# The drain of the last tiles of a fused attention and feed-forward layer: order, split copies, last layer norm

## The chip, the cores and the metric

The kernel runs on one core of one Trainium2 chip, as one launch. The time is the device time in microseconds, the median of several executions. TensorE (PE) multiplies, VectorE (DVE), ScalarE (ACT) and POOL (GpSimd) work element by element, SyncE (SP) issues the loads and stores of the token tiles. Each engine runs its own instructions in the order in which they were written, and waits on semaphores for the others.

## The reference

Input x is 16 x 512 tokens of width 256 in float32, 8192 tokens in all. All is float32.

```python
def favor(x):                       # per head of 16
    p = jnp.exp(x - jnp.max(x, axis=-1, keepdims=True))
    return p / (jnp.sum(p, axis=-1, keepdims=True) + 1e-6)

def fp4_linear(x, w):               # blocks of 16 along the last axis
    return jnp.einsum('bsk,nk->bsn', fp4_quant_dequant(x), fp4_quant_dequant(w))

x = layernorm(x + attention(x, Wq, bq, Wk, bk, Wv, bv, Wo, bo))   # linear attention on favor(q), favor(k)
h = jax.nn.silu(fp4_linear(x, w_gate)) * fp4_linear(x, w_up)      # width 704
x = layernorm(x + fp4_linear(h, w_down))                          # (x - mean) / sqrt(var + 1e-5)
```

`fp4_quant_dequant` scales each block of 16 by its largest absolute value over 6, rounds to the grid 0, 0.5, 1, 1.5, 2, 3, 4, 6 with its sign, and scales back. It is applied to the activations x and h as well as to the weights.

## The kernel before

The tokens are cut into 64 tiles of 128 (NT = 64), named n or, in sets of four, by sequence. The program has an attention part, which ends at about 240 us, and a feed-forward part. The array `res` holds the whole residual stream, 128 partitions x 64 tiles x 256, from the attention on. Every engine's program is written by one loop over steps m (`run`), and in a step each engine does one stage of several tiles: in step m of the feed-forward part TensorE does gate and up projections of tile m - 1 (in two halves, L974 and L996), the transposes of x of tile m (L981), the six transposes of the quantised hidden tile m - 4 (L992) and the down projection of tile m - 5 (L1001 to L1005). So steps 65 to 70 work off the last tiles, with ever fewer stages.

The way of one tile n from its hidden values to the output is the following, with the lines of the profile:

- VectorE finds the block maxima and their reciprocals (L759 to L769); POOL multiplies (L445); ScalarE squares and makes from it the rounding grid `hmg` (L606, L615); POOL adds the grid (L435) and VectorE subtracts it again (L808), which rounds to the FP4 grid; POOL multiplies by the scales (L416).
- TensorE transposes the six chunks into the PSUM tensor `wide` (L992). ScalarE copies them to `hqt_hi` rounded to the matmul's format (L594), VectorE subtracts that from `wide` to get the rest, `hqt_lo` (L814), and ScalarE copies a 64-row tail once more (L618, semaphore `h_dup`). The next tile's transposes wait for L618, since it reads `wide`.
- TensorE accumulates 17 matmuls of 128x256 into `bank5` (`pd`; L850, called by L1001, and L1003, L1005). It waits for `y_s`, the addition of the tile before, which frees the bank.
- VectorE adds the result to the residual and leaves the row sum (L772, `y_s`). ScalarE sums the squares about the mean (L492, `y_sq`).
- The layer norm's factors `rstd` and `nbias` are computed on VectorE for a batch of tiles at once, in thirteen small dependent steps (L643 to L657: an integer estimate of the inverse root, three Newton steps, the bias). The batches and the steps of the loop at which their operations stand are in `LN_B`: tiles 0 to 31, 32 to 47, 48 to 55, 56 to 59 and 60 to 63. The last starts at step 70, when the squares of tile 63 are there.
- ScalarE normalises each tile (L497) into one of four buffers `o_t`, and SyncE stores it (L336). `ready` spreads the normalisations of a batch over the steps behind its factors. They stand at the head of a step, ahead of the copy L594 of the same step. A normalisation also waits for the store that last read its buffer.

## Time and profile before

| what | value |
|---|---|
| median of 3 runs | 693.11 us (692.76 to 693.99) |
| the profiled execution | 694.08 us, its span 692.4 us |
| busy over the span | PE 673.5, DVE 634.7, ACT 572.7, POOL 575.9 us |
| granted TensorE clock, mean | 0.993 of full speed |
| stores | 64 of 128 KB, 1.7 us (median) from issue to landing |

The profile is of one execution. Its span is the time from the first to the last recorded event. Busy time is the sum of an engine's instructions; the chain of waits follows back from the last instruction what released each; a granted clock of 1.00 is 2.4 GHz. In the rows below a start is given in us from the span's start, and neighbouring instructions of one engine may overlap by about 0.1 us.

```profile
PE 673.5 (97%) x5586; PEld 640.9 (93%) x5586; DVE 634.7 (92%) x1499; ACT 572.7 (83%) x1356; POOL 575.9 (83%) x583
PE   8999999999999899999999999999999999999993
DVE  5999999999999879998999999899999999999884
ACT  6899999987779968898777768777777999888896
```

These are the busy times and 40 slices of the span, each digit the busy share of 17.3 us in tenths. The last slice is the drain of the pipeline.

### The profile page before, as it was taken

What the parts mean: (1) busy time and instruction counts of PE and PEld (TensorE: products, weight loads), DVE (VectorE), ACT (ScalarE), POOL (GpSimd) and SP (SyncE); (2) the same over time, 40 slices, a digit from 0 to 9 for tenths busy, and PEclk for the clock granted to TensorE, in tenths of its full rate; (3) what the DMA queues carried; (4) which work ended last, traced back from release to release, by engine and by line L of the source; (5) the groups of instructions that cost most, each with busy time, mean ns of one, the idle gap of its engine ahead of it and who ended that gap; (6) DMA issues with size and microseconds to landing.
All of it is one profiled execution on the core that took longest, in us unless ns stands there. A gap on an engine that the chain in (4) does not pass through costs nothing.

```text
span 692.4 us, 18052 instructions
## 1 busy us (share of the span) xinstructions
PE 673.5 (97%) x5586; PEld 640.9 (93%) x5586; DVE 634.7 (92%) x1499; ACT 572.7 (83%) x1356; POOL 575.9 (83%) x583
## 2 busy tenths in 40 slices
PE   8999999999999899999999999999999999999993
PEld 5899999999888799999999999999999999999983
DVE  5999999999999879998999999899999999999884
ACT  6899999987779968898777768777777999888896
POOL 5888888888888759998898899889878999888760
PEclk9999999999999999999999999999999999999998
DMA  5332323232331000000000000000000111101213
GB/s 159 101 91 75 98 73 92 84 94 78 92 91 58 18 1 0 3 1 1 1 2 1 2 1 1 2 1 1 2 1 2 46 40 39 47 32 47 69 60 116
DMA packets 40053, 29.87 MB, mean 43 GB/s; under 512 B 3731, under 2 KB 39958, under 8 KB 39958
## 3 DMA queue, kind: packets, MB, share of 16 engines
q1 hardware_dynamic: 37216, 26.49, 12.5%
q10 hardware_dynamic: 2742, 2.23, 1.1%
q8 instruction: 45, 0.74, 0.4%
q14 instruction: 50, 0.41, 0.2%
HBM read 20.32 MB, written 8.39 MB: 41 GB/s over the span
## 4 chain that ended last, share of the span: by engine, by line
PE 82%; issue 5%; POOL 5%; ACT 4%; DVE 3%; DMA 1%; ACTq 0%; SPq 0%; POOLq 0%; DVEq 0%
PE bank L850 62%; PE wide L992 6%; PE wide L850 5%; PE bank L981 2%; PE bank L932 2%; PE wide L950 1%; PE bank L912 1%; POOL scratch L399 1%; POOL scratch L374 1%; PE bank L1005 1%; PE bank L1003 1%; POOL rounded L391 1%; ACT scratch L497 1%; ACT dump L492 1%; DMA scratch<-L_attn_Wk 1%
## 5 line engine op out<-in xcount | busy, mean ns | idle before, releaser
L850 PE MATMUL bank<-wf_hi,rounded 128*128 128x352 f32 (+1 forms) x1664 | 387.2, 311 | 1.9 <-DVE res L772 1.7
L850 PEld LDWEIGHTS bank<-wf_hi,rounded 128*128 128x128 f32 x1664 | 284.4, 190 | 3.0 <-DVE rounded L814 1.7
L850 PE MATMUL bank<-wf_lo,rounded 128*128 128x352 f32 (+1 forms) x832 | 255.4, 307 | 0.0
L850 PEld LDWEIGHTS bank<-wf_lo,rounded 128*128 128x128 f32 x832 | 157.9, 190 | 0.0
L850 PE MATMUL bank<-qkv_hi,rounded 128*128 128x512 f32 (+1 forms) x512 | 144.7, 349 | 1.3 <-ACT bank L465 0.7
L435 POOL TENSOR_TENSOR scratch<-scratch 128x704 bf16<-128x704 f32 x64 | 98.6, 1541 | 16.2 <-ACT scratch L615 13.7
L445 POOL TENSOR_TENSOR scratch<-scratch 128x704 f32<-128x704 f32 x64 | 94.5, 1476 | 17.7 <-DVE scratch L769 16.9
L850 PEld LDWEIGHTS bank<-qkv_hi,rounded 128*128 128x128 f32 x512 | 91.8, 190 | 15.0 <-ACT bank L469 2.1
L416 POOL TENSOR_TENSOR scratch<-scratch 128x704 f32<-128x704 bf16 x64 | 89.1, 1392 | 19.0 <-DVE scratch L808 19.0
L399 POOL TENSOR_TENSOR scratch<-scratch 128x512 f32<-128x512 f32 x64 | 67.9, 1061 | 24.2 <-DVE scratch L748 24.0
L850 PE MATMUL bank<-qkv_lo,rounded 128*128 128x512 f32 (+1 forms) x256 | 87.1, 340 | 0.0
L575 ACT ACTIVATE scratch<-bank 128x352 f32<-128x352 f32 x64 | 29.5, 461 | 61.6 <-PE bank L850 61.3
L492 ACT ACTIVATE dump<-res,row_sum 128x256 f32<-128x256 f32 x128 | 64.5, 504 | 3.8 <-DVE res L772 3.4
L814 DVE TENSOR_TENSOR rounded<-wide,rounded 128x768 fp32r<-128x768 f32 x64 | 60.5, 946 | 2.0 <-ACT rounded L594 2.0
L850 PE MATMUL wide<-rounded 128*128 128x256 f32 x384 | 60.6, 294 | 0.9 <-DVE res L715 0.9
L606 ACT ACTIVATE scratch<-scratch 128x704 uint8<-128x704 f32 x64 | 50.4, 788 | 9.0 <-POOL scratch L445 8.9
L786 DVE TENSOR_TENSOR scratch<-scratch,bank 128x352 f32<-128x352 f32 x64 | 33.1, 517 | 24.4 <-ACT scratch L575 24.1
L992 PE MATMUL wide<-ident,scratch 128*128 128x128 f32 x384 | 52.5, 273 | 2.9 <-POOL scratch L416 1.5
L594 ACT ACTIVATE rounded<-wide 128x768 fp32r<-128x768 f32 x64 | 51.9, 811 | 3.8 <-PE wide L992 0.2
L850 PEld LDWEIGHTS wide<-rounded 128*128 128x128 f32 x384 | 51.1, 191 | 2.3 <-issue 1.2
L850 PEld LDWEIGHTS bank<-qkv_lo,rounded 128*128 128x128 f32 x256 | 48.9, 191 | 4.1
L411 POOL TENSOR_TENSOR scratch<-scratch 128x256 f32<-128x256 bf16 x64 | 50.3, 786 | 2.5 <-DVE scratch L778 2.5
(112 smaller groups left out, 1560.6 us busy)
## 6 DMA issues: line engine op xcount, KB each, us to landing
scratch<-x_feat SPq DMA_DIRECT2D x64, 128.0 KB, 2.3
scratch<-x_tok SPq DMA_DIRECT2D x64, 128.0 KB, 2.3
out<-scratch SPq DMA_DIRECT2D x64, 128.0 KB, 1.7
scratch<-w_ffn ACTq DMA_DIRECT2D x15, 128.0 KB, 2.1
scratch<-L_attn_Wq SPq DMA_DIRECT2D x1, 256.0 KB, 3.7
scratch<-L_attn_Wk SPq DMA_DIRECT2D x1, 256.0 KB, 3.9
scratch<-L_attn_Wv SPq DMA_DIRECT2D x1, 256.0 KB, 4.2
wo<-L_attn_Wo SPq DMA_DIRECT2D x1, 256.0 KB, 4.0
```

Source lines behind the costliest of these rows:

```text
L399: pool.tensor_tensor(features(n), prob[n % 2][:, :, 0:HD].rearrange("p (s h) d -> p s h d", s=2), over(hrec[n % 2], 2 * NH, HD).rearrange( ...
L411: pool.tensor_tensor(blocks(xq[:, n % T * D:(n % T + 1) * D]), blocks(e_g[e][:, half]), over(e_s2[p % 3][:, scales], XB), ALU.mult).then_i ...
L416: pool.tensor_tensor(hq[n % 2][:, 0:I].rearrange("p (a c e) -> p a c e", a=11, e=BLK), hg[n % 2].rearrange("p (a c e) -> p a c e", a=11, e ...
L435: pool.tensor_tensor(hc[n % 2], hxn[n % 2], hmg[n % 2], ALU.add).then_inc(h_c, 1)
L445: pool.tensor_tensor(blocks(hxn[n % 2]), blocks(hid[n % 2]), over(binv[n % 2], NB), ALU.mult).then_inc(h_xn, 1)
L492: act.activation(dump[norm][:, :], res[:, rows(n)], ACT.Square, bias=row_sum[:, at], scale=-1.0 * D, accum_out=row_sq[:, at]).then_inc(sq, 1)
L594: act.activation(hqt_hi[n % 2][:, :, :], wide[:, 0:IP].rearrange("p (c n) -> p c n", c=IC), ACT.Copy).then_inc(h_hi, 1)
L606: act.activation(hy[n % 2], hxn[n % 2], ACT.Square, scale=BOWL).then_inc(h_y, 1)
L786: dve.tensor_tensor(hid[n % 2][:, 0:HALF], gated[0], pu[0][:, 0:HALF], ALU.mult).then_inc(h_a, 1)
L814: dve.tensor_tensor(hqt_lo[n % 2][:, :, :], wide[:, 0:IP].rearrange("p (c n) -> p c n", c=IC), hqt_hi[n % 2][:, :, :].bitcast(F32), ALU.su ...
L850: op = pe.matmul(dst, x(c), w(c), start=first and n == 0, stop=last and n == len(terms) - 1, skip_group_check=not first)
L992: last = pe.transpose(wide[:, c * P:(c + 1) * P], hq[n % 2][:, c * P:(c + 1) * P], ident[:, :])
```

## The change

Nothing is changed before step 65, other than one memset of a constant on POOL at the start. From there:

- Tile 63's grid is added by VectorE (after-line L873) in place of POOL's L435.
- In steps 66 and later the small steps of the layer norm stand behind VectorE's subtraction L814 (now L883) of the same step, not ahead of it.
- Tile 63's transposes are signalled in two parts, four chunks and two; ScalarE's copy and VectorE's subtraction are two instructions each, and the down projection of tile 63 starts on the first part. It goes to `bank4`, and does not wait for the addition of tile 62.
- Tiles 48 to 63 are normalised in place in `res` and stored from there. `ACT_OUT` and `DVE_OUT` say at which step which tile is normalised by ScalarE and by VectorE (50, 56 to 59, 62, 63 are VectorE's), at the end of the step. `STORES` is the order of their stores.
- The last batch's layer norm has six steps on VectorE (`last_norm`): a square root on ScalarE (L659), its reciprocal, one Newton step, the bias. The square root's table is loaded at step 67 by a one-element activation (L655).

```diff
@@ -50,6 +50,13 @@
...
 SQUARE_AT = tuple(range(9, 41)) + tuple(61 + k * 2 // 3 for k in range(32))
+IN_PLACE = 48
+SQRT_AT = 69
+DRAIN = 65
+ROOT_OPS = 6
+ACT_OUT = {65: (48,), 66: (49,), 67: (51, 52, 53), 68: (54,), 69: (55,), 72: (60, 61)}
+DVE_OUT = {66: (50,), 68: (56, 57), 69: (58, 59), 72: (62, 63)}
+STORES = (48, 49, 50, 51, 52, 53, 56, 57, 54, 58, 59, 55, 62, 60, 63, 61)
 LN_B = ((0, 32, 2, 38), (32, 16, 2, 54), (48, 8, 4, 62), (56, 4, 7, 66), (60, 4, 7, 70))
...
@@ -206,7 +215,8 @@
         pg, pu = [bank[0], bank[2]], [bank[1], bank[3]]
-        pxt, pd = bank[4], bank[5]
+        pxt = bank[4]
+        pd = [bank[5]] * (NT - 1) + [bank[4]]
...
@@ -254,6 +264,17 @@
+        wide_c = wide[:, 0:IP].rearrange("p (c n) -> p c n", c=IC)
+        def h_parts(n):
+            return [slice(0, 4), slice(4, IC)] if n == NT - 1 else [slice(0, IC)]
+        def ln_done(n):
+            g = max(g for g, batch in enumerate(LN_B) if batch[0] <= n)
+            return LN_OPS * (g + 1) if g < len(LN_B) - 1 else LN_OPS * g + ROOT_OPS
@@ -335,8 +356,17 @@
...
-            for i in range(0, NS):
+            for i in range(0, IN_PLACE // T):
                 stores(i)
+            by_act, by_dve = IN_PLACE, 0
+            for m in STORES:
+                if any(m in tiles for tiles in DVE_OUT.values()):
+                    by_dve += 1
+                    sp.wait_ge(y_od, by_dve)
+                else:
+                    by_act += 1
+                    sp.wait_ge(y_o, by_act)
+                sp.dma_start(out[bass.ds(m * P, P), :], res[:, rows(m)]).then_inc(st_out[m % T], 16)
             for t in range(T):
...
@@ -429,6 +460,8 @@
                 for n in tile(m - 2):
+                    if n == NT - 1:
+                        continue
                     need(pool, h_xn, n + 1)
@@ -563,8 +596,9 @@
...
                 for g, n in ready(m, LN_B):
-                    need(act, st_out[n % T], 16 * (n // T))
-                    normalise(n, o_t[n % T], y_ln, LN_OPS * (g + 1), y_o)
+                    if n < IN_PLACE:
+                        need(act, st_out[n % T], 16 * (n // T))
+                        normalise(n, o_t[n % T], y_ln, LN_OPS * (g + 1), y_o)
                 for n in tile(m - 1):
@@ -589,10 +623,10 @@
...
                         act.wait_ge(a_qlo, NT)
-                    need(act, h_t, n + 1)
                     need(act, d_s, n - 1)
-                    act.activation(hqt_hi[n % 2][:, :, :], wide[:, 0:IP].rearrange("p (c n) -> p c n", c=IC),
-                                   ACT.Copy).then_inc(h_hi, 1)
+                    for k, part_ in enumerate(h_parts(n)):
+                        need(act, h_t, n + 1 + k)
+                        act.activation(hqt_hi[n % 2][:, part_, :], wide_c[:, part_, :], ACT.Copy).then_inc(h_hi, 1)
                 for p in pairs(m + 3):
@@ -614,9 +648,18 @@
...
                 for n in tile(m - 4):
-                    need(act, h_lo, n + 1)
+                    need(act, h_lo, n + len(h_parts(n)))
                     act.activation(hqt_hi[n % 2][TAIL:P, IC - 1, :], wide[0:TAIL, (IC - 1) * P:IP],
                                    ACT.Copy).then_inc(h_dup, 1)
+                if m == SQRT_AT - 2:
+                    act.activation(silu_at[:, :], eps[:, :], ACT.Sqrt)
+                if m == SQRT_AT:
+                    last, count = LN_B[-1][0:2]
+                    act.wait_ge(y_sq, NT)
+                    act.activation(ln_root[:, 0:count], row_sq[:, NT + last:NT + last + count], ACT.Sqrt,
+                                   bias=eps[:, :], scale=1.0 / D ** 3).then_inc(y_root, 1)
+                for n in ACT_OUT.get(m, ()):
+                    normalise(n, res[:, rows(n)], y_ln, ln_done(n), y_o)
@@ -656,6 +699,26 @@
...
+            def last_norm():
+                n, count = LN_B[-1][0:2]
+                at, stat = slice(n, n + count), slice(NT + n, NT + n + count)
+                v, r, t_, u = (x[:, 0:count] for x in (ln_v, ln_root, ln_t, ln_u))
+                y = rstd[:, at]
+                done = LN_OPS * (len(LN_B) - 1)
+                dve.wait_ge(y_sq, NT)
+                dve.wait_ge(y_ln, done)
+                dve.tensor_scalar(v, row_sq[:, stat], 1.0 / D ** 3, LN_EPS, ALU.mult, ALU.add).then_inc(y_ln, 1)
+                dve.wait_ge(y_root, 1)
+                dve.reciprocal(y, r).then_inc(y_ln, 1)
+                dve.wait_ge(y_ln, done + 2)
+                dve.scalar_tensor_tensor(t_, y, -0.5, y, ALU.mult, ALU.mult).then_inc(y_ln, 1)
+                dve.wait_ge(y_ln, done + 3)
+                dve.tensor_tensor(u, t_, v, ALU.mult).then_inc(y_ln, 1)
+                dve.wait_ge(y_ln, done + 4)
+                dve.scalar_tensor_tensor(y, u, 1.5, y, ALU.add, ALU.mult).then_inc(y_ln, 1)
+                dve.wait_ge(y_ln, done + 5)
+                dve.scalar_tensor_tensor(nbias[:, at], row_sum[:, stat], -1.0 / D, y, ALU.mult, ALU.mult).then_inc(y_ln, 1)
...
@@ -769,7 +832,7 @@
                     need(dve, d_s, n + 1)
-                    dve.scalar_tensor_tensor(res[:, rows(n)], pd[:, 0:D], SHY ** -4, res[:, rows(n)], ALU.mult, ALU.add,
+                    dve.scalar_tensor_tensor(res[:, rows(n)], pd[n][:, 0:D], SHY ** -4, res[:, rows(n)], ALU.mult, ALU.add,
                                              accum_out=row_sum[:, NT + n:NT + n + 1]).then_inc(y_s, 1)
@@ -792,27 +855,36 @@
...
                                       xqt_hi[n % 2][:, :, :].bitcast(F32), ALU.subtract).then_inc(x_lo, 1)
-                ln(0, m)
-                ln(1, m)
+                if m <= DRAIN:
+                    ln(0, m)
+                    ln(1, m)
                 for p in pairs(m + 5):
...
                     dve.reciprocal(e_inv[p % 2], e_s2[p % 3]).then_inc(e_invs, 1)
-                ln(2, m)
-                ln(3, m)
+                if m <= DRAIN:
+                    ln(2, m)
+                    ln(3, m)
                 for n in tile(m - 3):
...
                         dve.wait_ge(a_res, NT - 2 + n)
+                    if n == NT - 1:
+                        need(dve, h_mg, n + 1)
+                        dve.tensor_tensor(hc[n % 2], hxn[n % 2], hmg[n % 2], ALU.add).then_inc(h_c, 1)
                     need(dve, h_c, n + 1)
...
                         dve.wait_ge(a_out, NT)
-                    need(dve, h_hi, n + 1)
                     need(dve, d_s, n - 1)
-                    dve.tensor_tensor(hqt_lo[n % 2][:, :, :], wide[:, 0:IP].rearrange("p (c n) -> p c n", c=IC),
-                                      hqt_hi[n % 2][:, :, :].bitcast(F32), ALU.subtract).then_inc(h_lo, 1)
+                    for k, part_ in enumerate(h_parts(n)):
+                        need(dve, h_hi, n + 1 + k)
+                        dve.tensor_tensor(hqt_lo[n % 2][:, part_, :], wide_c[:, part_, :],
+                                          hqt_hi[n % 2][:, part_, :].bitcast(F32), ALU.subtract).then_inc(h_lo, 1)
+                if m > DRAIN:
+                    for k in range(4):
+                        ln(k, m)
                 for n in tile(m - 1):
@@ -832,6 +904,12 @@
...
                     dve.tensor_tensor(hid[n % 2][:, HALF:I], gated[1], pu[1][:, 0:HALF], ALU.mult).then_inc(h_b, 1)
+                if m == SQRT_AT + 1:
+                    last_norm()
+                for n in DVE_OUT.get(m, ()):
+                    need(dve, y_ln, ln_done(n))
+                    dve.tensor_scalar(res[:, rows(n)], res[:, rows(n)], rstd[:, n:n + 1], nbias[:, n:n + 1],
+                                      ALU.mult, ALU.add).then_inc(y_od, 1)
@@ -988,21 +1066,29 @@
...
                     need(pe, h_dup, n)
-                    for c in range(IC):
-                        last = pe.transpose(wide[:, c * P:(c + 1) * P], hq[n % 2][:, c * P:(c + 1) * P], ident[:, :])
-                    last.then_inc(h_t, 1)
+                    for part_ in h_parts(n):
+                        for c in range(part_.start, part_.stop):
+                            last = pe.transpose(wide[:, c * P:(c + 1) * P], hq[n % 2][:, c * P:(c + 1) * P], ident[:, :])
+                        last.then_inc(h_t, 1)
                 for n in tile(m - 1):
...
                     need(pe, h_lo, n + 1)
-                    need(pe, y_s, n)
-                    three(pd[:, 0:D], lambda c: hqt_hi[b][:, c, :], lambda c: hqt_lo[b][:, c, :],
-                          down(wf_hi), down(wf_lo), IC - 1, last=False)
-                    pe.matmul(pd[:, 0:D], hqt_lo[b][:, IC - 1, :], down(wf_hi)(IC - 1), start=False, stop=False)
+                    if n < NT - 1:
+                        need(pe, y_s, n)
+                        three(pd[n][:, 0:D], lambda c: hqt_hi[b][:, c, :], lambda c: hqt_lo[b][:, c, :],
+                              down(wf_hi), down(wf_lo), IC - 1, last=False)
+                    else:
+                        three(pd[n][:, 0:D], lambda c: hqt_hi[b][:, c, :], lambda c: hqt_lo[b][:, c, :],
+                              down(wf_hi), down(wf_lo), 4, last=False)
+                        need(pe, h_lo, n + 2)
+                        three(pd[n][:, 0:D], lambda c: hqt_hi[b][:, c + 4, :], lambda c: hqt_lo[b][:, c + 4, :],
+                              lambda c: down(wf_hi)(c + 4), lambda c: down(wf_lo)(c + 4), IC - 5, first=False, last=False)
+                    pe.matmul(pd[n][:, 0:D], hqt_lo[b][:, IC - 1, :], down(wf_hi)(IC - 1), start=False, stop=False)
                     need(pe, h_dup, n + 1)
-                    pe.matmul(pd[:, 0:D], hqt_hi[b][:, IC - 1, :], down(wf_hi)(IC - 1),
+                    pe.matmul(pd[n][:, 0:D], hqt_hi[b][:, IC - 1, :], down(wf_hi)(IC - 1),
                               start=False, stop=True).then_inc(d_s, 1)
```

VectorE at the steps 66 and 67, from the addition of tile 60 (the first L772) to that of tile 61 (the last), before; what stands left of an arrow is written, b_yln and the like are the semaphores waited for:

```order
L772 SCALAR_TENSOR_TENSOR res,row_sum<-bank5,res 128x256 [waits b_d]
L643 TENSOR_SCALAR ln_v<-row_sq 128x4 [waits b_ysq,a_x1]
L647 TENSOR_SCALAR ln_h<-ln_v 128x4 [waits b_yln]
L649 TENSOR_SCALAR rstd<-ln_h 128x4 [waits b_yln]
L653 SCALAR_TENSOR_TENSOR ln_t<-rstd 128x4 [waits b_yln]
L808 TENSOR_TENSOR scratch<-scratch 128x704 [waits b_hq,b_hc]
L814 TENSOR_TENSOR rounded<-wide,rounded 128x768 [waits b_d,b_hhi]
L655 TENSOR_TENSOR ln_u<-ln_t,ln_v 128x4 [waits b_yln]
L657 SCALAR_TENSOR_TENSOR rstd<-ln_u,rstd 128x4 [waits b_yln]
L772 SCALAR_TENSOR_TENSOR res,row_sum<-bank5,res 128x256 [waits b_d]
```

and in the changed kernel, where these lines are L835, L873 is the new addition of the grid, L876 is L808, L883 is L814 and L686 to L700 are L643 to L657:

```order
L835 SCALAR_TENSOR_TENSOR res,row_sum<-bank5,res 128x256 [waits b_d]
L873 TENSOR_TENSOR scratch<-scratch 128x704 [waits b_hmg]
L876 TENSOR_TENSOR scratch<-scratch 128x704 [waits b_hq,b_hc]
L883 TENSOR_TENSOR rounded<-wide,rounded 128x768 [waits b_hhi,b_d]
L686 TENSOR_SCALAR ln_v<-row_sq 128x4 [waits b_ysq,a_x1]
L690 TENSOR_SCALAR ln_h<-ln_v 128x4 [waits b_yln]
L692 TENSOR_SCALAR rstd<-ln_h 128x4 [waits b_yln]
L696 SCALAR_TENSOR_TENSOR ln_t<-rstd 128x4 [waits b_yln]
L698 TENSOR_TENSOR ln_u<-ln_t,ln_v 128x4 [waits b_yln]
L911 TENSOR_SCALAR res<-res,rstd,nbias 128x256 [waits b_yln]
L700 SCALAR_TENSOR_TENSOR rstd<-ln_u,rstd 128x4 [waits b_yln]
L835 SCALAR_TENSOR_TENSOR res,row_sum<-bank5,res 128x256 [waits b_d]
```

The subtraction of tile 62 moved ahead of all steps of the layer norm, and five of these, the normalisation of tile 50 (L911) and a sixth step now stand between it and the addition of tile 61.

ScalarE from the copy of tile 63's transposes (L594) on, before; L492 is the squares, L618 the tail copy, L497 the normalisations (tiles 56, 57, 58 ... in order):

```order
L594 ACTIVATE rounded<-wide 128x768 [waits b_d,b_ht]
L492 ACTIVATE dump1,row_sq<-res,row_sum 128x256 [waits b_y,b_ysq]
L618 ACTIVATE rounded<-wide 64x128 [waits b_hlo]
L497 ACTIVATE scratch<-res,nbias,rstd 128x256 [waits b_yln,st_out0]
L492 ACTIVATE dump1,row_sq<-res,row_sum 128x256 [waits b_y,b_ysq]
L497 ACTIVATE scratch<-res,nbias,rstd 128x256 [waits b_yln,st_out1]
L492 ACTIVATE dump1,row_sq<-res,row_sum 128x256 [waits b_y,b_ysq]
L497 ACTIVATE scratch<-res,nbias,rstd 128x256 [waits b_yln,st_out2]
L497 ACTIVATE scratch<-res,nbias,rstd 128x256 [waits b_yln,st_out3]
L497 ACTIVATE scratch<-res,nbias,rstd 128x256 [waits b_yln,st_out0]
L497 ACTIVATE scratch<-res,nbias,rstd 128x256 [waits b_yln,st_out1]
```

and in the changed kernel, where L629 is the copy, L525 the squares, L652 the tail copy, L530 the normalisations:

```order
L629 ACTIVATE rounded<-wide 128x512 [waits b_ht,b_d]
L629 ACTIVATE rounded<-wide 128x256 [waits b_ht]
L525 ACTIVATE dump1,row_sq<-res,row_sum 128x256 [waits b_y,b_ysq]
L652 ACTIVATE rounded<-wide 64x128 [waits b_hlo]
L655 ACT_TABLE_LOAD
L655 ACTIVATE silu_at<-eps 128x1
L530 ACTIVATE res<-res,nbias,rstd 128x256 [waits b_yln] x3
L525 ACTIVATE dump1,row_sq<-res,row_sum 128x256 [waits b_y,b_ysq]
L530 ACTIVATE res<-res,nbias,rstd 128x256 [waits b_yln]
L525 ACTIVATE dump1,row_sq<-res,row_sum 128x256 [waits b_y,b_ysq]
L659 ACTIVATE ln_root<-row_sq,eps 128x4 [waits b_ysq]
L530 ACTIVATE res<-res,nbias,rstd 128x256 [waits b_yln] x3
```

The copy is two instructions, a table load and its activation stand between the tail copy and the three normalisations of tiles 51, 52 and 53, the square root L659 stands behind the last squares, and of the last batch ScalarE normalises two tiles.

## Rows read from the trace of the kernel before

**Rows 1.** Of the windows of the tail: busy us (and instructions) by engine, granted clock, DMA.
```profile
665.00:672.00 7.00, 6.79 (x54) 6.58 (x52) 6.79 (x17) 6.76 (x15) 4.38 (x4) 1.00 0.17 59
...
684.00:692.40 8.40, 0.14 (x2) 0.00 (x0) 2.57 (x15) 3.66 (x8) 0.00 (x0) 0.63 0.31 108
```

**Rows 2.** The chain of waits, near its end: start us, us, what.
```profile
681.38 0.35 DVE res L772 x2
...
681.87 2.03 PE bank L850 x15
```

**Rows 3.** Timeline of ScalarE: start us, us, engine, line, op, tiles, count, idle before.
```profile
673.26 2.08 ACT L497 ACTIVATE scratch<-res,nbias,rstd 128x256 f32<-128x256 f32 x4
675.24 0.79 ACT L594 ACTIVATE rounded<-wide 128x768 fp32r<-128x768 f32 x1
...
677.06 0.27 ACT L618 ACTIVATE rounded<-wide 64x128 fp32r<-64x128 f32 x1 [0.54 <-DVE rounded L814]
677.35 2.08 ACT L497 ACTIVATE scratch<-res,nbias,rstd 128x256 f32<-128x256 f32 x4
...
684.71 0.51 ACT L492 ACTIVATE dump<-res,row_sum 128x256 f32<-128x256 f32 x1 [1.64 <-DVE res L772]
685.12 0.19 ACT L492 ACTIVATION_READ_ACCUMULATOR dump<-res,row_sum 128x1 f32 x1
...
688.06 2.07 ACT L497 ACTIVATE scratch<-res,nbias,rstd 128x256 f32<-128x256 f32 x4 [1.77 <-DVE nbias L651]
```

**Rows 4.** Timeline of VectorE, the same columns.
```profile
672.54 0.41 DVE L772 SCALAR_TENSOR_TENSOR res<-bank,res 128x256 f32<-128x256 f32 x1
...
675.12 0.53 DVE L808 TENSOR_TENSOR scratch<-scratch 128x704 bf16<-128x704 bf16 x1
676.07 0.96 DVE L814 TENSOR_TENSOR rounded<-wide,rounded 128x768 fp32r<-128x768 f32 x1 [0.42 <-ACT rounded L594]
...
677.31 0.42 DVE L772 SCALAR_TENSOR_TENSOR res<-bank,res 128x256 f32<-128x256 f32 x1
...
685.41 0.17 DVE L643 TENSOR_SCALAR ln_v<-row_sq 128x4 f32<-128x4 f32 x1 [0.80 <-ACT dump L492]
...
687.80 0.16 DVE L651 SCALAR_TENSOR_TENSOR nbias<-row_sum,rstd 128x4 f32<-128x4 f32 x1
```

**Rows 5.** Timeline of POOL, its last products.
```profile
673.24 1.53 POOL L435 TENSOR_TENSOR scratch<-scratch 128x704 bf16<-128x704 f32 x1
675.79 1.39 POOL L416 TENSOR_TENSOR scratch<-scratch 128x704 f32<-128x704 bf16 x1 [1.01 <-DVE scratch L808]
```

**Rows 6.** Timeline of TensorE, the last two tiles' transposes and down projections.
```profile
673.38 0.85 PE L992 MATMUL wide<-ident,scratch 128*128 128x128 f32 x6 [1.15 <-POOL scratch L416]
...
677.47 0.84 PE L992 MATMUL wide<-ident,scratch 128*128 128x128 f32 x6 [1.23 <-ACT rounded L618]
678.07 0.36 PE L850 MATMUL bank<-wf_hi,rounded 128*128 128x256 f32 x1
...
683.86 0.28 PE L1005 MATMUL bank<-wf_hi,rounded 128*128 128x256 f32 x1
```

**Rows 7.** Timeline of ScalarE around its second table load.
```profile
235.69 0.19 ACT L492 ACTIVATION_READ_ACCUMULATOR dump<-res,row_sum 128x1 f32 x1
235.90 1.28 ACT L508 ACT_TABLE_LOAD   x1
...
237.30 0.59 ACT L497 ACTIVATE res<-res,nbias,rstd 128x256 f32<-128x256 f32 x1
```

**Rows 8.** One line's instructions each: count, shortest, median and longest ns, first and last start.
```profile
L824 DVE TENSOR_TENSOR scratch<-scratch x32: 714/872/1172, 236.6 to 641.2; 128x512 bf16<-128x512 f32 x32
...
L562 ACT ACTIVATE rounded<-wide x16: 581/597/599, 27.6 to 238.5; 128x512 fp32r<-128x512 f32 x16
...
L582 ACT ACTIVATE rounded<-bank x64: 363/379/382, 242.1 to 658.2; 128x256 fp32r<-128x256 f32 x64
...
L336 SPq DMA_DIRECT2D out<-scratch x64: 332/332/964, 536.8 to 690.2; - x64
```

9 lines of the change are left out of this document (6 added, 3 removed).

## The prediction, as it went on record

> **What bounds the kernel now.** I read the table of stretches first. Until 672 us TensorE is busy 6.79 of 7 us; from 684 to the end it works 0.14 of 8.4 us [rows 1]. Everything the change edits is issued after 672, so the time in question is the tail, the last 20 us, and there a latency and not a busy share decides. The chain of waits says which [rows 2]: VectorE's addition of tile 62 to the residual at 681.38, then 2.03 us of matmuls of the last down projection, and then, as the engines' own rows show, the layer norm of the last four tiles and their normalisations. So I lined up the four engines' rows from 672 on and moved each instruction. "Down n", "copy n" are the down projection and the PSUM copy of tile n; all starts are us from the span's start.
>
> What the reader is to see in them:
> - Normalisations of finished tiles stand ahead of the copies. Four run from 673.26 for 2.08 us, and copy 62 starts at 675.24; four more from 677.35 hold up copy 63 in the same way [rows 3]. TensorE had written tile 62's transposes by 673.38 + 0.85 = 674.23 [rows 6], so copy 62 is 1 us late.
> - Down 63 starts at 681.87, 0.13 after the residual addition of tile 62 that frees its PSUM bank [rows 2], and ends at 683.86 + 0.28 = 684.14 [rows 6].
> - From there on it is a serial chain: addition, squares from 684.71 (their sum read back at 685.12 + 0.19 = 685.31), thirteen small VectorE operations from 685.41 to 687.96, four normalisations on ScalarE until 688.06 + 2.07 = 690.13, the last store issued at 690.2 [rows 3, 4, 8]. The span ends 2.2 us after that issue.
>
> **The change, part by part.** I carry it forward as the new time of each event, with the old one beside it.
>
> 1. Tile 63's addition of its rounding grid goes from POOL to VectorE. It can start at 672.99, behind the addition of tile 60 (672.54 + 0.41 [rows 4]). The trace has no such operation of 704 elements on VectorE. From above: POOL's, 1.53 us [rows 5]. From below: the 512-element one, at least 0.71 [rows 8]. I take 0.91 (the lower one and 192 more elements at about 1 ns): done at 673.9. The subtraction behind it ends at 674.4 (0.53 [rows 4]), POOL's product, 1.39 [rows 5], at 675.9 instead of 677.18. Worth nothing by itself, since part 2 is later; even 1.53 would leave it at 676.5.
>
> 2. Normalisations behind the copies. Copy 62 starts at 674.25 (one normalisation, tile 48, fits before it), 0.99 earlier; VectorE's subtraction ends at 676.04 instead of 677.03, the small copy L618 ends at 676.34 instead of 677.33 [rows 3, 4], and the transposes of tile 63, which wait for that copy, start at 676.48 instead of 677.47 [rows 6].
>
> 3. Down 62 does not follow. It needs the addition of tile 61 to free the bank, and down 61 is over at 676.24 (677.47 less the idle 1.23 [rows 6]). But the new order puts five small layer-norm steps, a normalisation of tile 50 and a sixth step between the subtraction of tile 62 and that addition. Those steps depend on each other: in the last layer norm the thirteenth starts 2.39 us after the first, 0.20 each [rows 4]. From 675.95, 0.28 for the first and 0.20 for the rest, the addition starts at 677.3, where it stands today (677.31 [rows 4]). Down 62 then starts at 677.85, against 678.07 [rows 6]: 1 us of lead shrinks to 0.2. Had the addition come first, down 62 would start at 677.1; that is the lower bound.
>
> 4. Copies in two parts, and bank 4 for down 63. Two pieces cost more than one: 0.60 + 0.38 on ScalarE [rows 8], less 0.1 of overlap, for 0.79. They start at 677.1 behind only four transposes, and all pieces on both engines are done by 679.1. That is before down 62 ends, 2.28 us after its start (678.07 to 680.07 + 0.28 in the same pattern as down 63's 1.99 + 0.28 [rows 6]): 680.1. So the split is hidden, and with its own bank down 63 follows at once, 2.0 to 2.1 us more: 682.2 instead of 684.14. **Term: -1.94.**
>
> 5. The table load. The square root needs one on ScalarE. The one in the trace: the instruction before it ends at 235.88, the load starts at 235.90, takes 1.28, and the next normalisation starts at 237.30, so 1.42 in all with the one-element activation [rows 7]. It starts at 679.1 and ends at 680.5 with that activation. Behind it stand three normalisations at 0.5 us, the squares of tile 62 (0.6), one normalisation (0.5), and only then the squares of tile 63, at 683.0 to 683.6. Their data are there at 682.75 (0.57 after down 63's end, as 684.14 to 684.71 before [rows 3]). So ScalarE, not TensorE, is late, by 0.25. **Term: +0.25.** The bound the other way: with no load, 0.
>
> The Trainium skill ("ScalarE: Activation LUTs", What ACT_TABLE_LOAD costs) puts about 1380 ns of drain on top of a 1283 ns load, 2.66 us for each switch. The trace agrees on the load (1283 ns) and shows 0.02 us of idle before it, no drain [rows 7]; by the page's figure the end would be 1.4 us later than my sum.
>
> 6. The last layer norm: seven steps fewer. From the squares' read-back: first step after 0.10, square root beside it, reciprocal, four dependent steps. 683.6 + 0.1 for the first; the root at 683.67 to 683.87 (0.20, the one-element activation [rows 7]), a hand-over of 0.08, then five at 0.20: factors ready at 684.9. That is 1.3 us behind the read-back where it was 2.65. **Term: -1.35.** Unknown are the 4-element root and reciprocal: between 0.16 (a small step [rows 4]) and 0.5 (a 256-wide activation) each, so -1.4 to -0.7.
>
> 7. Four normalisations become two on ScalarE and two on VectorE. ScalarE ends 0.10 + 1.08 behind the factors instead of 0.10 + 2.07. VectorE's, 256 wide, lie between 0.16 (4 elements) and 0.42 (the addition of the same width with PSUM) [rows 4]; I take 0.33: done before ScalarE at either end. **Term: -0.99.**
>
> 8. The stores. All four now become ready within 0.9 us. Before, the last was issued 0.07 after its data. A store holds SyncE's queue 0.33 [rows 8], 0.38 with its neighbours' gap (my guess from it). Issued at 685.4, 685.75, 686.1, 686.5, the last is 0.4 behind its data. **Term: +0.33.** The in-place writing frees ScalarE of waiting for old stores, which it did not do in the tail: nothing.
>
> The memset of the constant at the start stands in front of POOL work with slack; nothing.
>
> Sum: -1.94 + 0.25 - 1.35 - 0.99 + 0.33 = **-3.7 us**. Against the profiled execution (694.08: span 692.4 and 1.68 around it) that is a span of 688.7 and 690.4 in all. The median of the runs is 693.11, 0.97 under the profiled one; I predict 693.1 - 3.7 = **689.4**.
>
> **Rivals.**
> - A. The switch costs more than its row, by a wait of its own length again. Mechanism here: squares of tile 62 and 63 stand behind it on ScalarE, which is already the late engine, so all of 1.3 to 1.4 us reaches the end: 690.8. For: only one load in a loaded program is shown. Against: no gap in [rows 7]. Chance 0.12.
> - B. The lead of part 2 survives, because the small steps before the addition of tile 61 overlap more than 0.2 each, or ScalarE's queue is shorter than I add up. Down 63 ends up to 0.75 earlier, but ScalarE's queue then sets the squares, so at most 0.3 to 0.5 arrives, and the stores may issue without their gap (0.3): 688.7. Chance 0.2.
> - C. Slower: TensorE's clock falls in its gaps. The granted clock is 1.00 until 684 and 0.63 on average once the engine is idle behind it [rows 1]. If the gap before the transposes of tile 62 did that, at half the clock (1.2 instead of 2.4 GHz) downs 61, 62 and 63 would take twice their 2.0 us each: 689.4 + 6 = 695.4. It decides from the second slow down projection on (693.4). Against: today's gaps of 1.23 and 1.5 us leave it at 1.00, and the new ones (1.15, 0.24, 0.75) are shorter. Chance 0.03.
> - D. No visible effect: the order on the engines changes but something I did not see waits as long (the in-order stores, SyncE waiting for one of two counters at a time): 692 to 693. Against: every store's data but the last four are ready 1 us or more ahead. Chance 0.05.
>
> My forecast has 0.6. From these: faster by more than 0.2% (under 691.7; 0.2% is about what a measurement of this kernel can tell from no change) 0.92, within it 0.05, slower 0.03. The range runs from 688.4 (B with a root and reciprocal at their lower ends and a run at the low side of today's spread, 0.35) to 690.9 (A, or the upper ends of part 6).
>
> **What would show it.** In the profile of the changed kernel: copy 62 at 674.3; down 62 at 677.9 and not 677.1 (part 3), down 63 right behind it and over at 682.2; a load of 1.28 us on ScalarE at 679.1 and its squares of tile 63 starting at 683.0, with no idle time before them (part 5); factors at 684.9; ScalarE's last normalisation at 686.1; last store at 686.5; span 688.7. A gap around the load speaks for A, an idle ScalarE before the squares refutes part 5, a granted clock under 1 before 682 is C. I am wrong if the rows before 672 shift, for I assume that nothing there changes.

## The result, and the profile after

The kernel became slower. Times are device microseconds of whole executions.

| | median | lowest to highest | profiled execution | its span | mean granted clock |
|---|---|---|---|---|---|
| before | 692.82 | 692.17 to 693.99 (9 runs) | 694.08 | 692.4 | 0.993 |
| after | 695.14 | 694.08 to 695.72 (9 runs) | 694.54 | 692.5 | 0.997 |

The ratio after to before is 1.0032, with a 95% interval of 1.0023 to 1.0041: 2.3 us slower (1.6 to 2.8 by the interval). I had forecast 3.7 us faster. The ratios here and below are those on record; one can differ from the quotient of the two medians by 0.001.

The change touches only the last 20 us, so I first asked whether they became shorter. As a mark I took ScalarE's first gate activation of tile 63, an instruction far enough ahead of the drain to be untouched by it. In the timeline of ScalarE it stands here in before, and then in after (start us, us, engine, line, operation, tiles, count, idle before):

```profile
664.54 0.47 ACT L575 ACTIVATE scratch<-bank 128x352 f32<-128x352 f32 x1 [0.90 <-PE bank L850]
```

```profile
667.51 0.46 ACT L609 ACTIVATE scratch<-bank 128x352 f32<-128x352 f32 x1 [0.90 <-PE bank L928]
```

From that mark to the end of the span it is 27.8 us before (692.4 - 664.54, with more digits 27.81) and 25.0 after (24.98). The drain is 2.83 us shorter. But the mark itself is 2.97 us late. All of the gain, and more, was given back before the first changed instruction, in the tiles where I had assumed that nothing moves.

The steady tiles show how. This is the chain of waits of before in the middle of the transformer's feed-forward part (start us, us, what), and below it that of after:

```profile
604.78 3.70 PE bank L850 x27
...
608.72 1.92 PE bank L850 x12
...
611.51 3.70 PE bank L850 x27
```

```profile
607.03 3.77 PE bank L928 x27
...
611.05 1.93 PE bank L928 x12
...
613.85 3.77 PE bank L928 x27
```

The same matmuls in the same order. One tile takes 611.51 - 604.78 = 6.73 us before and 613.85 - 607.03 = 6.82 after. The lengthening sits in the piece of 27: twelve matmuls of 352 columns (the second half of gate and up) and fifteen of 256 (down). The twelve start 167 ns apart in the median instead of 158 (in the mean 166 instead of 159), the twelve of the first half 160 apart in both, and those of 256 columns 120 in both. The period, the median distance from tile to tile, is 6.733 and 6.813. Over the 55 tiles from number 9 to 63 that would be 55 x 0.08 = 4.4 us. By the marks of the tiles themselves, the first gate activations of tile 8 and of tile 63, it is 4.05, since tiles 43 to 48 are uneven in every trace and after lost less there, and 0.17 more is lost between tile 0 and tile 8.

It is not the clock and not the DMA. The table of stretches for 40 us of this part, before and then after (busy us and instructions of PE, PEld, DVE, ACT and POOL, granted clock, DMA share, GB/s):

```profile
300.00:340.00 40.00, 40.00 (x294) 39.88 (x293) 37.42 (x83) 34.38 (x82) 36.06 (x31) 1.00 0.00 1
```

```profile
300.00:340.00 40.00, 40.00 (x289) 39.90 (x288) 36.76 (x81) 33.55 (x78) 36.07 (x31) 1.00 0.01 1
...
672.00:684.00 12.00, 9.78 (x78) 9.01 (x77) 10.64 (x35) 10.16 (x23) 5.07 (x4) 1.00 0.20 66
...
684.00:692.50 8.50, 1.25 (x11) 1.04 (x9) 3.15 (x14) 4.73 (x12) 0.00 (x0) 0.72 0.61 201
```

TensorE is busy for all 40 us at a granted clock of 1.00 in both, and gets 289 matmuls done where it got 294. A busy share of 100% hides this completely; only the count, or the distance between starts, shows it. The last row answers to the last of [rows 1]: 1.25 us of TensorE where there were 0.14, since everything before the drain is late.

The spans alone (692.4 and 692.5) say less than the medians, because the profiled execution of before had a stretch that after's lacks. Before:

```profile
242.00:244.00 2.00, 1.69 (x8) 1.53 (x9) 1.40 (x5) 1.44 (x6) 1.84 (x4) 0.62 0.00 0
244.00:246.00 2.00, 2.00 (x10) 1.92 (x8) 0.98 (x3) 0.00 (x0) 1.32 (x2) 0.53 0.00 0
```

The granted clock was 0.62 and 0.53 for 4 us, where after has 1.00 in both. At tile 0 after is 1.25 us ahead, at tile 63 2.97 behind: from tile 0 to tile 63 the body takes 421.4 us instead of 417.2 and so lost 4.22, and the drain gave 2.83 back, which leaves a loss of 1.4.

One more term lies outside the span, where no row shows it. The time of a run is longer than its span by 1.7 us in the runs of before (694.08 for a span of 692.35) and by 2.02 to 2.09 in all nine of after (694.54 for 692.50), that is, by 0.3 more. So body, drain and this make 4.2 - 2.8 + 0.3 = 1.7 us slower. The medians say 2.3; the rest lies inside the interval.

Now the drain, which the prediction spoke of. Its times were to be shifted by those 2.97 us. ScalarE in the profile of after, answering to [rows 3]:

```profile
677.31 0.81 ACT L629 ACTIVATE rounded<-wide 128x768 fp32r<-128x768 f32 x1 [0.46 <-PE wide L1071]
...
682.11 0.27 ACT L652 ACTIVATE rounded<-wide 64x128 fp32r<-64x128 f32 x1 [0.40 <-DVE rounded L883]
682.39 1.28 ACT L655 ACT_TABLE_LOAD   x1
683.69 0.20 ACT L655 ACTIVATE silu_at<-eps 128x1 f32<-128x1 f32 x1
683.80 1.57 ACT L530 ACTIVATE res<-res,nbias,rstd 128x256 f32<-128x256 f32 x3
685.28 0.49 ACT L525 ACTIVATE dump<-res,row_sum 128x256 f32<-128x256 f32 x1
...
685.77 0.58 ACT L530 ACTIVATE res<-res,nbias,rstd 128x256 f32<-128x256 f32 x1
686.26 0.49 ACT L525 ACTIVATE dump<-res,row_sum 128x256 f32<-128x256 f32 x1
...
688.21 1.09 ACT L530 ACTIVATE res<-res,nbias,rstd 128x256 f32<-128x256 f32 x2 [0.54 <-DVE nbias L721]
```

From the small copy at 682.11 to the last squares at 686.26 ScalarE has no idle time: load, three normalisations, squares of tile 62, one normalisation, squares of tile 63. VectorE, answering to [rows 4]:

```profile
675.96 1.07 DVE L873 TENSOR_TENSOR scratch<-scratch 128x704 bf16<-128x704 f32 x1
...
680.37 0.41 DVE L835 SCALAR_TENSOR_TENSOR res<-bank,res 128x256 f32<-128x256 f32 x1
...
685.29 0.42 DVE L835 SCALAR_TENSOR_TENSOR res<-bank,res 128x256 f32<-128x256 f32 x1 [0.95 <-PE bank L1091]
...
686.88 0.17 DVE L711 TENSOR_SCALAR ln_v<-row_sq 128x4 f32<-128x4 f32 x1 [0.51 <-ACT dump L525]
...
688.01 0.16 DVE L721 SCALAR_TENSOR_TENSOR nbias<-row_sum,rstd 128x4 f32<-128x4 f32 x1
```

Tile 63's addition starts at 685.29 and its squares at 686.26, 0.97 later; before it was 0.52, with ScalarE idle. So the squares wait some 0.45 us for the engine. TensorE, answering to [rows 6], the first and last matmuls of downs 62 and 63:

```profile
680.94 0.36 PE L928 MATMUL bank<-wf_hi,rounded 128*128 128x256 f32 x1 [0.47 <-DVE res L835]
...
682.93 0.28 PE L1091 MATMUL bank<-wf_hi,rounded 128*128 128x256 f32 x1
683.05 0.28 PE L928 MATMUL bank<-wf_hi,rounded 128*128 128x256 f32 x1
...
684.97 0.28 PE L1091 MATMUL bank<-wf_hi,rounded 128*128 128x256 f32 x1
```

Down 63 now starts 0.12 us after the start of down 62's last matmul, the usual distance of these matmuls. And SyncE's queue of DMA issues, first before and then after:

```profile
688.68 1.81 SPq L336 DMA_DIRECT2D out<-scratch  x4
```

```profile
686.76 3.89 SPq L369 DMA_DIRECT2D out<-res  x8
```

After, the stores start 0.49 us apart with no gap; these eight are those that fall into the stretch asked for, and the unbroken row of ten begins earlier, at 685.78. Before, the last four also start 0.49 apart, but there each waits for its normalisation.

### The profile page after: what moved, and what is told of

It reads as the page before. It is cut to its first block, busy times and chain, and to the rows that moved or that the text cites. A ratio compares the mean times of both kernels' runs of the same rounds, so it can differ in the third digit from the quotient of the medians.

```text
span 692.5 us, 18033 instructions
## 1 busy us (share of the span) xinstructions
PE 677.2 (98%) x5586; PEld 644.8 (93%) x5586; DVE 631.5 (91%) x1501; ACT 571.9 (83%) x1353; POOL 573.8 (83%) x583
## 4 chain that ended last, share of the span: by engine, by line
PE 82%; POOL 5%; issue 5%; ACT 4%; DVE 3%; DMA 0%; ACTq 0%; POOLq 0%; DVEq 0%
PE bank L928 63%; PE wide L1071 6%; PE wide L928 5%; PE bank L1059 2%; PE bank L1010 2%; PE wide L1028 1%; PE bank L990 1%; POOL scratch L430 1%; POOL scratch L405 1%; PE bank L1091 1%; PE bank L1089 1%; POOL rounded L422 1%; ACT dump L525 1%; ACT res L530 1%; DVE rounded L883 0%
## 5 line engine op out<-in xcount | busy, mean ns | idle before, releaser
L468 POOL TENSOR_TENSOR scratch<-scratch 128x704 bf16<-128x704 f32 x63 | 96.7, 1535 | 22.2 <-ACT scratch L649 19.9
L525 ACT ACTIVATE dump<-res,row_sum 128x256 f32<-128x256 f32 x128 | 64.4, 504 | 1.1 <-DVE res L835 0.7
L883 DVE TENSOR_TENSOR rounded<-wide,rounded 128x768 fp32r<-128x768 f32 (+1 forms) x65 | 61.0, 939 | 1.5 <-ACT rounded L629 0.8
L629 ACT ACTIVATE rounded<-wide 128x768 fp32r<-128x768 f32 (+1 forms) x65 | 52.1, 802 | 6.3 <-PE wide L1071 6.2
```

The lines of the kernel that those rows point to most:

```text
L468: pool.tensor_tensor(hc[n % 2], hxn[n % 2], hmg[n % 2], ALU.add).then_inc(h_c, 1)
L525: act.activation(dump[norm][:, :], res[:, rows(n)], ACT.Square, bias=row_sum[:, at], scale=-1.0 * D, accum_out=row_sq[:, at]).then_inc(sq, 1)
L629: act.activation(hqt_hi[n % 2][:, part_, :], wide_c[:, part_, :], ACT.Copy).then_inc(h_hi, 1)
L883: dve.tensor_tensor(hqt_lo[n % 2][:, part_, :], wide_c[:, part_, :], hqt_hi[n % 2][:, part_, :].bitcast(F32), ALU.subtract).then_inc(h_lo, 1)
```

## The experiments

Two questions: what slows the body, and why the drain gave 2.83 and not 3.7 us. Where a time stands without an interval it is one run or the profiled execution's. "Mark" is the gate activation above. Sixteen kernels are variants of before or after; the seventeenth leaves the layer out.

### Is it the addresses?

The section on the change says that nothing is changed before step 65 other than a memset. That was wrong: the change also allocates two small tensors, `eps` and `ln_root`, behind `silu_at`, and so moves all tensors allocated later by 64 bytes in each partition (32 each, rounded up). No instruction of the steady tiles is edited. Theory L: the addresses slow TensorE. Rival: the code itself, through its waits or its size. The expectations put on record call them theory 1 and theory 2.

`a1_pad64`, the kernel before with two unused tensors:

```diff
         silu_at = sb("silu_at", [P, 1])
+        pad_a = sb("pad_a", [P, 1])
+        pad_b = sb("pad_b", [P, 4])
```

> The kernel before with two unused tensors allocated behind silu_at, so that the weights, scratch and rounded lie 64 bytes further on, as in the changed kernel; no instruction is changed. Theory 1 (the addresses): the feed-forward tile period goes from 6.73 to 6.81 us as in the changed kernel, and the time is 3.5 to 5 us above the kernel before (about 697). Theory 2 (the edited code, the early memset or the chip's state on the day): the time is that of the kernel before, within 0.7 us, and the period stays 6.73.

Measured: 697.48 (4 runs) against 692.56, ratio 1.0071 [1.0056, 1.0086]: 4.9 us slower, with a period of 6.81 us. From tile 0 to tile 63 its trace takes 421.4 us, as after's does, and before's 417.2. Two tensors that nobody reads cost what the body of after lost; the 4.2 us of the traces lie inside the interval of the runs, 3.9 to 6.0.

`a2_end`, the kernel after with its two tensors allocated last, all others at their old addresses:

```diff
-        eps = sb("eps", [P, 1])
-        ln_root = sb("ln_root", [P, T])
 ...
+        eps = sb("eps", [P, 1])
+        ln_root = sb("ln_root", [P, T])
```

> The changed kernel with eps and ln_root allocated behind all other tensors, so that every other tensor lies where it lay before; no instruction is changed. Theory 1 (the addresses): period 6.73 us, and the gain of the drain alone is seen, 3 to 4 us below the kernel before (about 689.3). Theory 2 (the edited code): still about 695, period 6.81.

Measured: 690.20 (8 runs), ratio 0.9969 [0.9959, 0.9979]: 2.4 us faster than before, period 6.73, and 417.0 us from tile 0 to tile 63. Its chain of waits:

```profile
603.99 3.70 PE bank L928 x27
...
607.93 1.92 PE bank L928 x12
...
610.72 3.70 PE bank L928 x27
```

The 3.70 is back. Together, +4.9 and -2.4 make +2.5, against +2.3 measured for the change. Theory L holds from both sides; the rival falls, as the same code runs at either period.

`a3_pad32` and `a4_pad128`, the kernel before shifted by other amounts (one unused tensor; one of 128 bytes):

> The kernel before with one unused tensor behind silu_at: a shift of 32 bytes (weights start at 64 over a multiple of 128, before at 32, changed kernel at 96). Theory 1a (any move off today's place costs): 2 to 5 us above before. Theory 1b (the cost depends on the place within 64 bytes or more in some regular way): some other value, possibly a period below 6.73. Theory 2: no change.

> The kernel before with an unused tensor of 128 bytes behind silu_at, so that all tensors behind keep their place modulo 128. Theory 1 in the form 'the place modulo 128 decides': time and period of the kernel before. In the form 'a longer modulus or the mutual distance to the tensors in front decides': up to 5 us more. Theory 2: no change.

Measured: ratios 1.0004 [0.9995, 1.0013] and 1.0005 [0.9996, 1.0015]. No change for either. So it isn't that tensors move, but where they start within 128 bytes: at 32 in before, 64 with the first shift, 32 with the second, 96 in after. Of these places 96 alone is slow.

### Whose addresses?

TensorE reads two operands there, the weights (`wf_hi`, `wf_lo`) as the moving one and the activations (`rounded`) as the stationary one; VectorE, ScalarE and POOL work in `scratch`. Each variant below is the kernel before with unused 64-byte tensors put so that only the named ones start at 96 instead of 32, for instance (`b3_rounded`):

```diff
+        pad_a = sb("pad_a", [P, 16])
         rounded = ...
```

> The kernel before with 64 unused bytes ahead of wf_hi and 64 more ahead of scratch: the feed-forward weights wf_hi and wf_lo start at 96 over a multiple of 128, as in the changed kernel, and scratch and rounded keep their place modulo 128. If the right-hand operand of TensorE's matmuls (the weights) is what must not lie there: tile period 6.81 us, time about 697. If another tensor is at fault: 6.73 and about 692.7.

> The kernel before with 64 unused bytes ahead of scratch and 64 more ahead of rounded: only scratch, which VectorE, ScalarE and POOL work in and from which TensorE takes the hidden tile to be transposed, lies at 96 over a multiple of 128. If these engines' accesses get in TensorE's way from there: period 6.81, about 697. Otherwise 6.73, about 692.7.

> The kernel before with 64 unused bytes ahead of rounded: only the left-hand operands of TensorE (xqt and hqt, high and low parts) lie 64 bytes further on. If loading them is what costs: period 6.81, about 697. Otherwise 6.73, about 692.7.

> The kernel before with unused bytes so that wf_hi, wf_lo and scratch start at 96 over a multiple of 128 and rounded at 32. With each of the three alone at 96 the period was 6.73, 6.73 and 6.64 us, with all three 6.81, so the places act together. If what counts is whether TensorE's two operands (weights and rounded) lie alike: here they differ the other way round than in b3, period 6.64 to 6.73, about 690. If scratch against rounded counts: as b3's pair, 6.64. If only the total of all three does harm: 6.73.

> The kernel before with unused bytes so that wf_hi, wf_lo and rounded start at 96 and scratch at 32. If the alike place of TensorE's two operands at 96 is what slows: period 6.81, about 697. If scratch must be there as well: 6.73 or below.

> The kernel before with 64 unused bytes ahead of scratch: scratch and rounded start at 96, the weights at 32. If TensorE's operands must differ for the fast period: 6.64, about 688.5. If scratch and rounded must differ: 6.73 or above.

Measured, one run each (start modulo 128; two values of the period where tiles alternate):

| weights | scratch | rounded | time | span | period |
|---|---|---|---|---|---|
| 32 | 32 | 32 (before) | 692.6 to 693.2 (two medians) | 692.4 | 6.73 |
| 96 | 32 | 32 | 690.38 | 688.7 | 6.73, from tile 50 on 6.64 |
| 32 | 96 | 32 | 691.79 | 690.1 | 6.73 and 6.72 |
| 32 | 32 | 96 | 688.41 | 686.7 | 6.64, from tile 50 on 6.64 and 6.73 |
| 96 | 96 | 32 | 688.45 | 686.7 | 6.64 |
| 32 | 96 | 96 | 690.61 | 688.9 | 6.64 and 6.73, from tile 48 on 6.73 |
| 96 | 32 | 96 | 694.53 | 692.8 | 6.72 and 6.82 |
| 96 | 96 | 96 (`a1_pad64`) | 697.48 | 695.8 | 6.81 |

No one tensor is to blame: with only one at 96 each single run was faster than before, for `scratch` alone by little (691.79 against 692.36, the lowest run of before beside it). The four rows where weights and activations start at different places are the four fastest, and the two slowest are those with both at 96. In the profile of `b3_rounded`, the same stretch as above:

```profile
300.00:340.00 40.00, 40.00 (x297) 39.87 (x296) 37.65 (x81) 33.94 (x80) 37.53 (x32) 1.00 0.00 1
```

297 matmuls where before has 294 and after 289. There the 256-column matmuls are 113 ns apart and not 120.

But the table does not say that a layout has one period. `b1_wf` changes its own within one execution, with every address as it was:

```profile
300.00:340.00 40.00, 40.00 (x293) 39.88 (x292) 36.58 (x79) 33.53 (x79) 36.55 (x31) 1.00 0.00 1
...
600.00:640.00 40.00, 40.00 (x297) 39.88 (x297) 39.55 (x87) 34.36 (x73) 35.24 (x29) 1.00 0.12 41
```

Its 256-column matmuls are 118 ns apart up to 524 us and 113 from 536 us on. In between lie the uneven tiles from 43 on. So where the two operands lie differently, the order among the four fastest rows can be chance; what switches the period was not tested. That a move would make the kernel faster, as `b3_rounded` did, neither reading on record had expected.

`h1_alone` measures this by itself. It leaves the layer out: TensorE runs 12 matmuls of 352 columns and 17 of 256, about the second part of a tile but without the transposes ahead of it, seven times in each of twelve stretches, with either operand at 32 (`mva` moving, `sta` stationary) or 96 (`mvb`, `stb`), the other engines first idle and then reading memory at 32 or 96.

```diff
+                for r in range(REP):
+                    for h in range(2):
+                        for k in range(6):
+                            pe.matmul(bank[h][:, 0:352], stn[:, k * 128:k * 128 + 128], mv[:, 352 * (k % 3):352 * (k % 3) + 352],
+                                      start=k == 0, stop=k == 5)
+                    for k in range(17):
+                        at = k % 8
+                        pe.matmul(bank[2][:, 0:256], stn[:, at * 128:at * 128 + 128], mv[:, 256 * (k % 5):256 * (k % 5) + 256],
+                                  start=k == 0, stop=k == 16)
```

> A kernel of its own that leaves the layer out and stores one tile of matmul results 64 times. TensorE runs 7 times the pattern of a tile (12 matmuls of 352 columns, 17 of 256) in twelve stretches: right-hand operand and left-hand operand each at 32 or at 96 over a multiple of 128, in all four pairs, first with the other engines idle, then with VectorE, ScalarE and POOL reading 512-wide rows of a tensor at 32, then at 96. If TensorE's own operands make the difference: the four stretches with the others idle differ by 1 to 6 per cent (0.113 against 0.120 us for 256 columns, 0.158 against 0.167 for 352). If it needs the other engines: the first four are alike and the last eight differ. If the order of the layer's own work makes it: all are alike.

Measured: 423.87 us in all, one run. The windows of four stretches (busy us and matmuls of TensorE, clock, DMA), in order: 32 against 96 (`mva`, `stb`), 96 against 32 (`mvb`, `sta`), both at 96 (`mvb`, `stb`), and again `mva` with `stb`, now with the other engines at work:

```profile
37.90:65.30 27.40, 27.36 (x205) 1.00 0.00 1
65.60:93.40 27.80, 27.80 (x205) 1.00 0.00 1
93.70:121.60 27.90, 27.89 (x204) 1.00 0.00 1
290.10:317.40 27.30, 27.28 (x204) 1.00 0.01 1
```

The median distance of 256-column matmuls was 114 ns for `mva` with `stb`, 118 for `mvb` with `sta`, and 120 for both pairs with equal places. The other engines made no difference to it, wherever they read. So with TensorE alone the places of its own two operands set this distance, and the 113 of `b3_rounded` (moving at 32, stationary at 96, as `mva` with `stb`) has its like here. In the layer more comes into it: `b1_wf` has the places of `mvb` with `sta` and shows both 118 and 113. And the 352-column matmuls stayed near 161 ns in all twelve stretches: the 167 ns that cost the change its gain are **not** reproduced. The slow ones of the layer stand directly behind the transposes, which this kernel does not have; that rival was not tested. In the layer both operands at 96 gave a period of 6.81 in all steady tiles with `scratch` at 96, and 6.72 and 6.82 by turns with it at 32, so `scratch` has a hand in it. What else it takes stays open.

`d1_before_rounded`, the kernel after with its two tensors allocated right ahead of `rounded`, so that only `rounded` starts at 96:

```diff
-        eps = sb("eps", [P, 1])
-        ln_root = sb("ln_root", [P, T])
 ...
+        eps = sb("eps", [P, 1])
+        ln_root = sb("ln_root", [P, T])
         rounded = ...
```

> The changed kernel with eps and ln_root allocated between scratch and rounded, so that rounded alone lies 64 bytes further on, as in b3. If the drain's gain and the layout's gain add up: 693 - 2.5 - 4.5, about 686, period 6.64. If the fast period of b3 was a chance of that one run: 690.

Measured: 687.46 (5 runs), ratio 0.9920 [0.9907, 0.9934]. 5.2 us faster than before; the same instructions as after, which is 2.3 slower. That is 1.5 more than the 686 expected. Its drain is that of after (25.00 us behind the mark), but its period is 6.64 and 6.73 by turns, though all three tensors lie at the very addresses of `b3_rounded`: 414.7 us from tile 0 to tile 63, where `b3_rounded` took 412.8.

### What bounds the drain?

Here the mark removes the body: all times are us behind it, read from the rows of each profiled execution.

| | tile 63's addition | its squares | ScalarE's last normalisation ends | last store issued | span ends |
|---|---|---|---|---|---|
| before | 19.64 | 20.16 | 25.59 | 25.61 | 27.81 |
| after | 17.77 | 18.75 | 21.79 | 22.69 | 24.98 |
| `a2_end` | 17.78 | 18.75 | 21.79 | 22.70 | 25.00 |
| `e1_first` | 17.20 | 18.74 | 21.78 | 22.71 | 25.00 |
| `e3_bank5` | 18.62 | 19.15 | 22.20 | 22.89 | 25.18 |
| `e2_newton` | 17.76 | 18.29 | 22.66 | 23.36 | 25.66 |
| `c1_two_queues` | 17.76 | 18.74 | 21.78 | 21.93 | 24.96 |
| `f1_best` | 17.32 | 18.02 | 21.08 | 21.32 | 23.93 |

The drain of `a2_end` is that of after to within 0.02, so it depends on the code and not on the layout, and serves as the base of the next four. Theory S: the down projections no longer matter; ScalarE's queue behind the table load sets the last squares, and SyncE's queue of issues the end. Rival T, called theory L in the expectations here: TensorE's chain of downs still sets it, as before.

`e1_first`: the layer-norm steps of the drain behind the additions of tiles 61 and 62 instead of ahead of them, the lower bound of the prediction's part 3.

```diff
-                ln(5, m - 1)
+                if m - 1 <= DRAIN:
+                    ln(5, m - 1)
 ...
                                              accum_out=row_sum[:, NT + n:NT + n + 1]).then_inc(y_s, 1)
+                if m - 1 > DRAIN:
+                    for k in range(6):
+                        ln(k, m - 1)
 ...
-                if m > DRAIN:
-                    for k in range(4):
-                        ln(k, m)
 ...
-                ln(4, m)
+                if m <= DRAIN:
+                    ln(4, m)
```

> a2_end (690.2 us) with VectorE's small layer-norm steps of steps 66 and 67 put behind the residual additions of tiles 61 and 62, so that down 62 no longer waits for them. Both theories: down 62 starts 0.6 to 0.8 us earlier and so does down 63. Theory L (the late down projection bounds the drain, part 3 of the prediction): the end comes 0.5 to 0.8 earlier, 689.6. Theory S (ScalarE's queue behind the table load, and SyncE's issue queue behind it, bound the drain): no gain, 0 to 0.2 later, 690.2 to 690.4.

Measured: 690.43 (10 runs), ratio 0.9972 [0.9963, 0.9982]. Down 62 starts earlier and the addition of tile 63 comes 0.58 us sooner; the squares, and the end, do not move. ScalarE's row:

```profile
681.27 0.49 ACT L525 ACTIVATE dump<-res,row_sum 128x256 f32<-128x256 f32 x1
...
681.77 0.58 ACT L530 ACTIVATE res<-res,nbias,rstd 128x256 f32<-128x256 f32 x1
682.26 0.49 ACT L525 ACTIVATE dump<-res,row_sum 128x256 f32<-128x256 f32 x1
```

No idle time ahead of any of them: the engine is full. T would have given the 0.58 to the end.

`e3_bank5`: down 63 in bank 5 again, waiting for tile 62's addition, that is, part 4's own bank taken back.

```diff
-        pd = [bank[5]] * (NT - 1) + [bank[4]]
+        pd = [bank[5]] * NT
```

> a2_end with down 63 in bank5 again, so that it waits for the addition of tile 62. Down 63 ends 0.7 us later in both theories. Theory L: the end 0.7 later, 690.9. Theory S: ScalarE has 0.4 us of lateness of its own that hides it, the end 0.1 to 0.3 later, 690.4.

Measured: 690.28 (6 runs), ratio 0.9967 [0.9954, 0.9981]. The addition of tile 63 comes 0.84 later than in `a2_end`, the squares 0.40, the last issue 0.19, the end 0.18. Of a wait of 0.84 us one fifth arrives: first ScalarE's lateness absorbs it, then the issue queue.

`e2_newton`: no root and no table load, the last layer norm with its thirteen steps again.

```diff
-                if m == SQRT_AT - 2:
-                    act.activation(silu_at[:, :], eps[:, :], ACT.Sqrt)
 ...
+                for k in range(LN_OPS):
+                    layer_norm(k, len(LN_B) - 1, LN_B, 1, y_ln, y_sq)
```

> a2_end with the last layer norm by thirteen VectorE steps as before: no square root, no table load. Theory S: the squares of tile 63 start 0.4 us sooner, the factors come 0.9 later (0.4 sooner, 1.35 more steps), the last store 0.6 later, 690.8. Theory L: the load cost nothing, the factors and the end come 1.3 us later, 691.5.

Measured: 690.14 (7 runs), ratio 0.9972 [0.9961, 0.9983]. The squares come 0.46 sooner, 0.53 behind the addition as they should when ScalarE is free: that is the load's whole price inside the span. But from the squares to the factors it is 1.34 more, and the end is 0.66 later. The whole time does not show that, nor the 690.8 expected: outside the span the seven runs take 1.71 to 1.77 us, as before's do, and those of `a2_end` 2.00 to 2.10. All seven kernels with the square root have the longer time there and no other has it, so root and load cost 0.3 us more that the rows do not show; why is open. By the whole time these three kernels cannot be told apart (0.3 us between their medians); the rows can.

`c1_two_queues`: the stores of VectorE's seven tiles issued by POOL.

```diff
+            for k, m in enumerate(m for m in STORES if any(m in tiles for tiles in DVE_OUT.values())):
+                pool.wait_ge(y_od, k + 1)
+                pool.dma_start(out[bass.ds(m * P, P), :], res[:, rows(m)]).then_inc(st_pool, 16)
```

> The changed kernel with eps and ln_root at the end, and the stores of the seven tiles that VectorE normalises issued by POOL, which is idle by then, the other nine by SyncE. In the changed kernel's trace eleven stores follow each other on SyncE 0.49 us apart, and the last is issued 0.9 us after ScalarE's last normalisation. Theory Q (SyncE's issue rate of one store per 0.49 us bounds the end): the last store of SyncE is issued within 0.1 us of its data and the time falls by 0.7 to 0.9 us against a2_end (690.2 to about 689.4), unless POOL's stores land later than SyncE's. Theory D (the landing of the stores is what takes the time, whoever issues them): no gain, 690.2.

Measured: 689.85 (4 runs), ratio 0.9957 [0.9941, 0.9974], but behind the mark it ends at 24.96, no gain. Its last issue is 0.77 us sooner (21.93 against 22.70), and POOL's stores take longer to land. The profile's list of DMA issues (KB each, median us from issue to landing), and POOL's last two:

```profile
out<-res SPq DMA_DIRECT2D x9, 128.0 KB, 1.8
...
out<-res POOLq DMA_DIRECT2D x7, 128.0 KB, 2.3
```

```profile
684.26 1.07 POOL L480 DMA_DIRECT2D out<-res  x2 [1.51 <-DVE res L910]
```

Half a microsecond for each issue and 2.3 to land eat what the shorter queue gave. Neither theory held as it was worded: the queue is what delays SyncE's last issue, and yet it alone does not set the end. The median is 0.35 below that of `a2_end`, within the spread of the runs.

`f1_best` puts together what the rows point to: the layout of `d1_before_rounded`, the order of `e1_first`, the load behind two normalisations instead of ahead of three, one normalisation moved from ScalarE to VectorE and two behind the last squares, and the store of tile 61 issued by ScalarE, so that SyncE's last is that of tile 63.

```diff
-ACT_OUT = {65: (48,), 66: (49,), 67: (51, 52, 53), 68: (54,), 69: (55,), 72: (60, 61)}
-DVE_OUT = {66: (50,), 68: (56, 57), 69: (58, 59), 72: (62, 63)}
+ACT_OUT = {65: (48,), 66: (49,), 67: (51, 52), 69: (54, 55), 72: (60, 61)}
+DVE_OUT = {66: (50,), 68: (53, 56, 57), 69: (58, 59), 72: (62, 63)}
 ...
+            act.dma_start(out[bass.ds((NT - 3) * P, P), :], res[:, rows(NT - 3)]).then_inc(st_out[(NT - 3) % T], 16)
```

> d1_before_rounded (687.46 us, 0.992 of before) with the order of e1, the table load behind two normalisations in place of ahead of three, tile 53 given to VectorE, tile 54 behind the last squares, and the last store issued by ScalarE's own queue. Theory S with the issue queue as the bound: the last store is issued 0.5 to 0.9 us earlier relative to tile 63's first gate activation than in d1, the time about 686.7. If the end is bound by anything else: no change against d1.

Measured: 685.01 (4 runs), ratio 0.9899 [0.9884, 0.9914]: 7.7 us faster than before, the best kernel of this study. Against `d1_before_rounded` it gained 2.45 us where 0.8 was expected. By the two traces the drain is 1.07 shorter, and the stretch from tile 0 to tile 63 is 1.9 shorter, where its period was 6.64 up to tile 42 and not 6.64 and 6.73 by turns. No run shows that the edits did the second, and the edits of the drain were not tried one by one. Its drain is 1.05 us shorter than after's; its load is over before tile 62's squares are wanted:

```profile
675.10 1.28 ACT L662 ACT_TABLE_LOAD   x1
...
676.51 0.49 ACT L525 ACTIVATE dump<-res,row_sum 128x256 f32<-128x256 f32 x1
...
677.12 0.51 ACT L525 ACTIVATE dump<-res,row_sum 128x256 f32<-128x256 f32 x1
...
680.21 0.35 ACTq L666 DMA_DIRECT2D out<-res  x1
```

## Why the prediction was wrong

The step that failed is the assumption at its end, and in its first paragraph: "Everything the change edits is issued after 672", "I assume that nothing there changes". What the change issues is late; what it allocates is there from the start. Two lines of the diff that I read as declarations moved every tensor of the steady tiles from 32 to 96 modulo 128, and the body lost 4.2 us by the traces and 4.9 by the runs of `a1_pad64`. None of my rivals held such a case, so my 0.03 for slower rested on the clock alone. The range missed by 4.2 us. With the addresses kept (`a2_end`) the same prediction would have met 690.2, inside its range, but with a gain of 2.4 us for the 3.7 forecast.

A second term stood at nothing without a reason: I took the 1.68 us around the span (1.73 with more digits) as fixed. They became 2.04, and `e2_newton` ties the 0.3 to the square root and its load.

The working on the drain, by its steps, in us behind the mark so that the body stays out:

- Parts 1 and 2 held. VectorE's 704-element addition took 1.07 (taken 0.91, bounds 0.71 to 1.53). Copy 62 began at 677.31, for 674.25 + 2.97 = 677.22, and the transposes of tile 63 start at 679.62, for a predicted 676.48 + 2.97 = 679.45.
- Part 3 held. The addition of tile 61 stood at 680.37, for 677.3 + 2.97 = 680.27, and down 62 at 680.94, for 680.82. The lead was indeed lost to the layer-norm steps; `e1_first` shows that it would have been lost anyway, on ScalarE.
- Part 4 held: down 63 directly behind down 62, tile 63's addition 1.87 earlier (term -1.94).
- Part 5 was right in kind and too small. The load took 1.28, with 0.01 us before it; ScalarE was the late engine, by 0.46 and not 0.25: `e2_newton` gives the 0.46 back. The three normalisations took 1.57 and the fourth 0.58, and the load itself began 0.3 later than in my sum (682.39, for 679.1 + 2.97): the pieces of copy and subtraction were done at 682.07, just as I had them, but the small copy L652, 0.27 long, stands between them and the load, and I had left it out. Rival A, a switch that costs its length twice, is refuted: the first normalisation starts 1.41 behind the load's start, 1.40 in [rows 7]. What the square root and its load cost beyond that, 0.3, lies outside the span.
- Part 6 was exact in its sum, -1.35, with some luck: the root took 0.30 for my 0.20, and the hand-overs around it less than I had. The reciprocal took 0.18; both lie inside 0.16 to 0.5.
- Part 7: -1.04 for -0.99.
- Part 8 was mis-sized. I took 0.33 for each issue from the median of [rows 8], where each store waits for its data, and 0.38 from one to the next. Issued directly behind each other they hold the queue 0.44 to 0.45 and start 0.49 apart, so the last goes out 0.90 behind its data instead of 0.4. The term is +0.88 instead of +0.33. Three distances of 0.49 instead of 0.38 are 0.33 of the difference. I had also counted the four stores of the last batch alone, but the unbroken row starts at 685.78, before that batch's factors are ready (688.01 + 0.16 = 688.17): older stores held the first of the four by about 0.1.
- What comes behind the last issue took 0.09 longer.

The sum is -1.87 + 0.46 - 1.35 - 1.04 + 0.88 + 0.09 = -2.83 inside the span, and -2.5 with the 0.3 outside it, for my -3.7. Rival B gave the drain more, and it got less. Rival C did not come: the granted clock is 1.00 from 672 to 684. Rival D did not either, by `a2_end`.

Left open: why twelve matmuls in 41 start 167 ns apart when weights, scratch and activations all start at 96; what lets one layout run at two periods; and where the 0.3 us outside the span are spent. That the addresses slow the body is shown; the way in which they do is not.

## What to carry to other kernels

Two declarations are a change to everything allocated behind them: before anything is predicted from the edited code, compare the addresses, and put new small tensors last. Where TensorE is busy all the time, count its matmuls in a fixed stretch, for a busy share of 100% looks the same at 289 and at 297. Compare the time of a run with its span as well, for what lies outside it shows in no row. And an instruction's shortest duration is not its price in a row: whoever makes four results ready at once must price the queue that carries them away. A layout that made a single run faster is not yet a faster layout: look whether the period holds through the trace and in a second kernel.

## What the runs showed of the hardware

- With TensorE alone the distance of 256-column matmuls depends on where the two operands start within 128 bytes: 114 and 118 ns where they differ (32 and 96), 120 where they are equal. In the layer it was 113 to 118 ns where they differ, both within one execution of `b1_wf`, and 118.5 to 120 in the mean where they are equal. In the layer the placements tried span 688.4 to 697.5 us.
- With weights, activations and the other engines' scratch all at 96, the 352-column matmuls behind the transposes were 167 ns apart instead of 158. In the kernel without the layer, which has no transposes, those of 352 columns were 161 to 162 apart wherever the operands lay.
- Of after's sixteen stores of 128 KB, five held SyncE's queue 0.33 to 0.34 us; those had waited for their data. The eleven whose data were ready held it 0.43 to 0.45, and in an unbroken row they follow each other every 0.49. Shortest, median and longest in ns:

```profile
L369 SPq DMA_DIRECT2D out<-res x16: 332/444/452, 676.9 to 690.2; - x16
```

- The same store issued by POOL took 0.54 us of the engine (0.75 the first of seven) and 2.3 to land, against 1.8 from SyncE.
- The time of a run beyond its span was 1.68 to 1.78 us in all runs of before and of its variants, and 2.00 to 2.10 in those of the seven kernels that load the square root's table in the drain; `e2_newton`, the same without it, has 1.71 to 1.77.
